# First quartet routed and sent in round 3 of attention, and GpSimd keeping at most two scattered transfers under way

## The chip, the cores and the metric

The kernel runs on one core of one Trainium2 chip. The metric is the device time of that core in microseconds, the median of several runs.

## The reference

16 sequences of 128 tokens with 128 features go through one layer of cross-attention and one layer of mixture of experts. Cut to what matters:

```python
x = x + xattn(layernorm(x), ctx, ctx, mask, Wq, Wk, Wv, Wo)   # 16 heads of 8, a softmax over 128 keys
x = x + moe(layernorm(x), wg, w1, w3, w2)                     # 8 experts, hidden size 256

# moe:
probs = softmax(x @ wg.T)
topk_w, topk_idx = top_k(probs, 2)
topk_w = topk_w / sum(topk_w)
y_e = (silu(x @ w1[e].T) * (x @ w3[e].T)) @ w2[e].T
out = sum over the two chosen experts of topk_w * y_e
```

## The kernel before, in words

**Attention.** The 16 sequences are four quartets of four. A loop over `u` from 0 to 4 runs the rounds. Round `u` starts quartet `u` (projections of queries and keys, first scores, whose row maxima VectorE takes from PSUM, L1356) and finishes quartet `u-1` (second scores with the maximum folded in, L649 and L652, exponentials on ScalarE, L905, product with the values, L627, and the projection out). Counted from 0, round 3 (`u == 3`, `u + 1 == NQ`) is the last that starts a quartet, and the last round is `u == 4`. A round has 20 ticks, `tick = 4*b + g`, with `b` from 0 to 4 and `g` from 0 to 3. Each engine's instructions are written out by hand in order of ticks, and engines meet through semaphores alone. The maxima of round `u` are turned (`MT`), copied (`mT`, L1256) and spread by GpSimd into `m_bd` (L989), which the second scores of round `u+1` read.

**Routing.** When a quartet has left attention, VectorE takes its statistics (`second_statistics`, L1043 and L1048), GpSimd the inverse deviation (`inverse_deviation`), VectorE writes the normalised rows twice each (`normalise`, L1068), TensorE turns them (`fill(("x2T", q))`) and multiplies them with the gate (`("lg", q)`), ScalarE copies (`prepare`), and VectorE ranks the experts in three steps (`routing_step`, L1154 to L1174). TensorE counts how many earlier tokens chose the same expert (`("rk", q)`, L550 and L552), `place_rows` (L1179 to L1186) turns this into row numbers, and `weigh` into weights (with `squash` on ScalarE). GpSimd then scatters the quartet's rows, eight transfers of 128 rows of 129 words, to `xg` in DRAM (`send`, L1003). The work banks of PSUM are handed round in the order of `slot_order`, built from the list `LAST_FILLS`.

**Experts.** Quartets 0 to 2 make the first phase, with 31 tiles of 128 rows, and quartet 3 the second, with 15. SyncE clears the tails of the regions (L446), waits for `sent` and loads the tiles (L464). Per tile TensorE turns it (L692), multiplies it into the hidden layer (L705 to L708), turns the result (L718) and multiplies it down (L731, L732); VectorE sums the halves into `y_sb` (`take_rows`, L1379); GpSimd scatters it to `ys` (L1016). 15 input and 14 output buffers rotate. Quartet 3 is routed while the first tiles run: from tile 8 on GpSimd sends two transfers of it after each of four tiles. Before the last round's second scores TensorE turns the first expert weights (`("W", 0)` to `("W", 3)`) and does `("rk", 0)`.

**GpSimd's order** is: `m_bd` of the round, the inverse deviations, `m_bd` of the last round, the inverse deviation of quartet 2, then the sends of quartets 0, 1 and 2, and then the tiles.

Of the kernel before, what the change touches and what calls it, by code (L numbers as in the profile page):

```python
# [47 lines left out]
QB = 4  # L48
# [35 lines left out]
def constants():  # L84
# [29 lines left out]
    for j in range(NJ):  # L114
# [10 lines left out]
LAST_FILLS = {-1: [("W", 0), ("W", 1), ("W", 2), ("W", 3), ("rk", 0)], 0: [("W", 4), ("x2T", 1)], 1: [("W", 5)], 2: [("lg", 1)],  # L125
              3: [("W", 6)], 4: [("x2T", 2)], 5: [("W", 7)], 6: [("rk", 1), ("lg", 2)], 10: [("rk", 2)], 11: [("cn", 0)],
# [8 lines left out]
def slot_order():  # L135

    order = ["w", ("cT", 0), ("xT", 0)]
    for u in range(NQ):
        order += [("V", u)]
        if u:  # L140
            order += [("MT", u - 1)]
        order += [("st", u, k) for k in range(2 * NG)]
        if u == 0:
            order += ["wo"]
        order += [("cT", u + 1), ("xT", u + 1)] if u + 1 < NQ else [("x2T", 0), ("lg", 0)]
# [25 lines left out]
def program(nc, x, ctx_in, mask, Wq, Wk, Wv, Wo, wg, w1, w3, w2, consts, xg, ys, out):  # L171
    slot, bank_of, turn, uses = slot_order()
    with ExitStack() as stack:
# [140 lines left out]
        sent = [sem(f"sent{q}") for q in range(NQ)]  # L314
# [80 lines left out]
        def _(sp):  # L395
# [43 lines left out]
            def open_phase(f):  # L439
# [10 lines left out]
                for q in (range(3) if f == 0 else range(3, NQ)):  # L450
                    sp.wait_ge(sent[q], 16 * 2 * QB)
# [28 lines left out]
        def _(pe):  # L480
# [154 lines left out]
            for u in range(NQ + 1):  # L635
                front(u)
                for b in range(QB + 1):
                    for g in range(NG):
# [39 lines left out]
                        if (b, g) == (3, 0) and u + 1 == NQ:  # L678
                            fill(("x2T", 0))
                        if (b, g) == (3, 3) and u + 1 == NQ:  # L680
                            fill(("lg", 0))
# [90 lines left out]
        def _(act):  # L772
# [76 lines left out]
            for u in range(NQ + 1):  # L849
# [31 lines left out]
                for b in range(QB + 1 if u else 0):  # L881
                    for g in range(NG):
# [6 lines left out]
                        if u == NQ:  # L889
                            for name in last_fills(NG * b + g - 1):  # L890
                                if name[0] == "W":
                                    take_weights(name[1])
                                if name[0] == "x2T":
                                    prepare(name[1])
                            if NG * b + g in (0, 5, 10):
                                squash((NG * b + g) // 5)
                        if u == NQ - 1 and (b, g) == (3, 1):
                            prepare(0)
# [48 lines left out]
        def _(pool):  # L947
# [31 lines left out]

            mask_context(0)  # L980
# [19 lines left out]
            def send(n, k):  # L1000

                f = n // QB // 3
                pool.indirect_dma_start(xg[f], bass.IndirectOffsetOnAxis(rows_i[:, n, k:k + 1], 0), sent_rows(n // QB)[:, n % QB, k, :],  # L1003
                                        None, bounds_check=E * REGS[f] - CT - 1, oob_is_err=False).then_inc(sent[n // QB], 16)

            inverse_deviation(NQ + 2)
            for q in range(3):
                pool.wait_ge(rows_ready, q + 1)
                for m in range(2 * QB):
                    send(QB * q + m // 2, m % 2)  # L1010
# [12 lines left out]

        @block.vector
        def _(dve):
# [33 lines left out]
            def normalise_batch(n0, m, b):  # L1059
                if b == 0:  # L1060
                    dve.wait_ge(rstd_ready, m + 1)
                    if m == NQ + 3:
                        dve.wait_ge(sent[0], 16 * 2 * QB)
# [185 lines left out]
            for u in range(NQ + 1):  # L1249
# [41 lines left out]
                for b in range(QB + 1):  # L1291
                    for g in range(NG):
                        if u < NQ:

                            n0, m = (QB * (u + 1), u + 1) if u + 1 < NQ else (0, NQ)
                            if (b, g) == (1, 0):
                                if u + 1 < NQ:
                                    dve.wait_ge(in_x[u + 1], 16)
                                else:
                                    dve.wait_ge(x2_done, QB)  # L1300
                            if b == 1:
                                row_statistics(n0, g)
                            if (b, g) == ((2, 0) if u + 1 < NQ else (1, 3)):
                                mean_variance(m)
                            if b == 2 and g in (1, 2) and u + 1 < NQ:
                                masks(u + 1, g - 1)
                            if b == (3 if u + 1 < NQ else 2):
                                normalise_batch(n0, m, g)
                            if u + 1 == NQ and (b, g) == (3, 0):
                                second_statistics(1)  # L1310
                            if u + 1 == NQ and b == 4:
                                if g < 3:
                                    routing_step(0, g)
                                else:
                                    normalise(QB, NQ + 1)
# [7 lines left out]
                        if u == NQ:  # L1323
# [5 lines left out]
                            if tick == 0:  # L1329
                                place_rows(0)  # L1330
                                second_statistics(2)
                            if tick == 1:
                                weigh(0)
                            if tick == 2:
                                normalise(2 * QB, NQ + 2)
                            if tick in (3, 4):
                                routing_step(1, tick - 3)
                            if tick == 5:
                                routing_step(1, 2)
                            if tick == 7:  # L1340
                                place_rows(1)
                                weigh(1)
                            if tick in (8, 9):
                                routing_step(2, tick - 8)
                            if tick == 10:
                                routing_step(2, 2)
                            if tick == 11:
                                place_rows(2)
                            if tick in (12, 13, 14):
                                table(0, tick - 12)  # L1350
                            if tick == 15:
# [91 lines left out]
```

## Time and profile before

| | |
|---|---|
| median of 3 runs | 327.69 us (327.08 to 329.23) |
| time of the profiled execution | 327.09 us |
| its span, first to last instruction | 325.3 us |
| mean granted TensorE clock | 0.871 |
| round 3 of attention (`u == 3`), its ticks | 112.6 to 142.3 us of the span |
| last round (`u == 4`) with its front | 142.3 to 202.5 us |
| expert tiles | 205.3 to 315.8 us |
| gather and output | 316 to 325.3 us |

The profiled execution took 1.8 us more than its span and 0.6 us less than the median. Times inside the kernel are counted from the start of the span. The chain of waits follows the work that ended last back to the start; what it calls another core or an unknown queue is time for which it found no releaser, and on one core there is no other core.

### The profile page before, as it was taken

What the parts mean: (1) busy time and instruction counts of PE and PEld (TensorE: products, weight loads), DVE (VectorE), ACT (ScalarE), POOL (GpSimd) and SP (SyncE); (2) the same over time, 40 slices, a digit from 0 to 9 for tenths busy, and PEclk for the clock granted to TensorE, in tenths of its full rate; (3) what the DMA queues carried; (4) which work ended last, traced back from release to release, by engine and by line L of the source; (5) the groups of instructions that cost most, each with busy time, mean ns of one, the idle gap of its engine ahead of it and who ended that gap; (6) DMA issues with size and microseconds to landing.
All of it is one profiled execution on the core that took longest, in us unless ns stands there. A gap on an engine that the chain in (4) does not pass through costs nothing.

```text
span 325.3 us, 5807 instructions
## 1 busy us (share of the span) xinstructions
PE 233.3 (72%) x1591; PEld 180.4 (55%) x1591; DVE 219.9 (68%) x642; ACT 141.8 (44%) x318; POOL 114.3 (35%) x125
## 2 busy tenths in 40 slices
PE   0946788889898988747564818679674698899820
PEld 0733565667566656546342606658563697789710
DVE  5597965887598758857734424387862586688983
ACT  6792256546655664206321406335220354455400
POOL 5201250125011502033737360035277264555540
PEclk9986599999999999957977566799985699999975
DMA  6995504450443044510301154102113134428006
GB/s 177 256 260 105 123 2 87 83 115 11 90 91 81 2 97 99 134 61 2 82 24 53 34 111 97 27 8 61 50 51 70 33 82 94 106 51 217 26 11 194
DMA packets 43886, 27.31 MB, mean 84 GB/s; under 512 B 5030, under 2 KB 41397, under 8 KB 43856
## 3 DMA queue, kind: packets, MB, share of 16 engines
q1 hardware_dynamic: 40208, 20.95, 28.2%
q0 software_dynamic: 2816, 5.27, 5.4%
q10 hardware_dynamic: 832, 0.72, 0.8%
q8 instruction: 14, 0.23, 0.3%
q14 instruction: 16, 0.13, 0.1%
HBM read 13.27 MB, written 7.37 MB: 63 GB/s over the span
## 4 chain that ended last, share of the span: by engine, by line
PE 41%; DVE 20%; issue 9%; another core or an unknown queue 8%; SPq 7%; DMA 7%; ACT 5%; POOL 2%; POOLq 0%; DVEq 0%; ACTq 0%
PE bank L493 6%; SPq L421 6%; PE bank L499 4%; DVE m_neg L1356 4%; DMA bd<-st 3%; PE bank L649 3%; PE bank L731 3%; PE bank L652 2%; PE bank L666 2%; PE bank L732 2%; PE bank L705 2%; PE bank L718 2%; PE bank L627 2%; PE bank L708 2%
## 5 line engine op out<-in xcount | busy, mean ns | idle before, releaser
L1016 POOL DMA_INDIRECT ys<-big x46 | 45.3, 986 | 41.5 <-DVE big L1379 22.6
L1356 DVE TENSOR_REDUCE m_neg<-bank 128x4 f32<-128x512 f32 x64 | 43.4, 685 | 18.1 <-PE bank L666 17.8
L905 ACT ACTIVATE big<-bank 128x512 f32<-128x512 f32 x64 | 37.5, 597 | 25.6 <-PE bank L652 24.0
L774 ACT ACTIVATE st<-bank 128x128 fp32r<-128x128 f32 (+1 forms) x92 | 26.3, 329 | 35.0 <-PE bank L718 12.9
L731 PE MATMUL bank<-bd,st 128*128 x92 | 28.1, 327 | 10.5 <-DVE big L1379 10.1
L649 PE MATMUL bank<-m_bd,ones_b 128*128 128x512 f32 x64 | 31.7, 496 | 3.7 <-ACT big L905 1.9
L666 PE MATMUL bank<-bd,st 128*128 128x512 f32 x64 | 29.1, 477 | 7.2 <-DMA bd<-st 5.8
L968 POOL TENSOR_SCALAR ve<-mv 128x4 f32<-128x4 f32 x8 | 1.8, 228 | 87.0 <-DVE mv L1048 87.0
L1398 DVE TENSOR_TENSOR big<-big,bank 128x256 f32<-128x256 f32 x46 | 19.3, 419 | 16.2 <-ACT big L937 13.6
L1283 DVE SCALAR_TENSOR_TENSOR st<-st_hi,cst,bank 128x512 fp32r<-128x512 f32 x32 | 23.3, 747 | 8.8 <-ACT st_hi L774 4.3
L937 ACT ACTIVATE big<-bank 128x256 f32<-128x256 f32 x46 | 17.7, 385 | 25.9 <-PE bank L708 13.1
L1003 POOL DMA_INDIRECT xg<-rows,rows_i x24 | 23.7, 986 | 12.2 <-issue 6.6
L705 PE MATMUL bank<-bd,st 128*128 x46 | 23.5, 510 | 6.0 <-DVE st L1367 2.9
L652 PE MATMUL bank<-bd,st 128*128 128x512 f32 x64 | 27.0, 423 | 0.0
L989 POOL TENSOR_TENSOR m_bd<-mT,cst 128x512 fp32r<-128x512 f32 x16 | 17.2, 1106 | 26.6 <-DVE mT L1256 26.6
L731 PEld LDWEIGHTS bank<-bd,st 128*128 128x128 f32 x92 | 18.2, 198 | 14.1 <-issue 12.4
L732 PE MATMUL bank<-bd,st 128*128 x92 | 24.9, 291 | 0.0
L1379 DVE TENSOR_REDUCE big<-bank 128x128 f32<-128x256 f32 x46 | 19.3, 419 | 5.8 <-remote 3.5
L1372 DVE TENSOR_TENSOR st<-bank,st 128x256 fp32r<-128x256 f32 x46 | 19.4, 422 | 4.7 <-issue 2.1
L666 PEld LDWEIGHTS bank<-bd,st 128*128 128x128 f32 x64 | 13.5, 215 | 13.2 <-issue 8.2
L774 ACT ACTIVATE onT<-bank 128x128 f32<-128x128 f32 x16 | 4.4, 276 | 37.3 <-PE bank L519 21.8
L706 PE MATMUL bank<-bd,st 128*128 x46 | 19.1, 415 | 0.0
(172 smaller groups left out, 566.4 us busy)
## 6 DMA issues: line engine op xcount, KB each, us to landing
bd<-st SPq DMA_DIRECT2D x128, 64.0 KB, 2.1
big<-xg SPq DMA_DIRECT2D x46, 64.5 KB
raw<-ys SPq DMA_DIRECT2D x8, 256.0 KB, 3.2
xg<-in_patterns SPq DMA_DIRECT2D x18, 64.5 KB
x_all<-in_x SPq DMA_DIRECT2D x4, 256.0 KB, 4.3
rows<-in_mask_BxS_if POOLq DMA_DIRECT2D x4, 256.0 KB, 5.0
ctx_all<-in_L_ffn_w SPq DMA_DIRECT2D x1, 1024.0 KB, 5.9
out<-ctx_all SPq DMA_DIRECT2D x4, 256.0 KB, 3.8
```

The lines of the kernel that those rows point to most:

```text
L649: nc.tensor.matmul(s2[k % 2][:, :], ones_b[:, b, :], m_bd[:, NJ * g:NJ * (g + 1), :].rearrange("p h q -> p (h q)"), start=True, stop=False)
L652: nc.tensor.matmul(s2[k % 2][:, :], st[:, (u - 1) % 2, 1, g, b * S:(b + 1) * S], bd_slot(0, n)[:, g, :, :].rearrange("p j q -> p (j q)"), ...
L666: nc.tensor.matmul(s1[k % s1_ring(u)][:, :], st[:, u % 2, 0, g, (b - 1) * S:b * S], bd_slot(1, n)[:, g, :, :].rearrange("p j q -> p (j q)" ...
L705: nc.tensor.matmul(both, t_lo[n % 2], first_high[:, :, bass.ds(col[n], I)], start=True, stop=False)
L731: nc.tensor.matmul(o, g_hi[n % GR][:, c * P:(c + 1) * P], w, start=(c == 0), stop=False)
L732: last = nc.tensor.matmul(o, g_lo[n % GR][:, c * P:(c + 1) * P], w, start=False, stop=(c == 1))
L774: return nc.scalar.activation(o, i, ACT.Copy)
L905: nc.scalar.activation(prob[n % 2][:, NJ * g:NJ * (g + 1), :].rearrange("p h q -> p (h q)"), s2[k % 2][:, :], ACT.Exp, scale=SCALE).then_i ...
L1003: pool.indirect_dma_start(xg[f], bass.IndirectOffsetOnAxis(rows_i[:, n, k:k + 1], 0), sent_rows(n // QB)[:, n % QB, k, :], None, bounds_ch ...
L1016: pool.indirect_dma_start(ys[f], bass.IndirectOffsetOnAxis(xt[n % XR][:, D:RW].bitcast(I32), 0), y_sb[n % YR], None, bounds_check=2 * CAPS ...
L1283: nc.vector.scalar_tensor_tensor(st[:, u % 2, is_k, g, :], st_hi[:, n % SH, :].bitcast(F32), cst[:, (C_CK if is_k else C_CQ):(C_CK if is_k ...
L1356: nc.vector.tensor_reduce(m_neg[:, H * (b - 1) + NJ * g:H * (b - 1) + NJ * (g + 1)], s1[k % s1_ring(u)][:, :].rearrange("p (j q) -> p j q" ...
```

## The change

Quartet 0's statistics move to tick 19 of round `u == 2`. Its normalisation, gate, three routing steps, count, rows and weights move to ticks 0 to 14 of round `u == 3`, and its eight transfers are issued by GpSimd there, ahead of `m_bd` of the last round. Quartet 1 comes a few ticks earlier: it is normalised at ticks 11 and 12 of `u == 3` and starts its ranking at tick 19. Quartet 2 gets its rows at tick 10 of the last round and not at tick 11. GpSimd gets waits: transfer `n` of a quartet waits until transfer `n-2` has landed, each scatter of a tile waits until that of two tiles before has landed, and quartet 3 is sent with one transfer after each of eight tiles.

```diff
-LAST_FILLS = {-1: [("W", 0), ("W", 1), ("W", 2), ("W", 3), ("rk", 0)], 0: [("W", 4), ("x2T", 1)], 1: [("W", 5)], 2: [("lg", 1)],
-              3: [("W", 6)], 4: [("x2T", 2)], 5: [("W", 7)], 6: [("rk", 1), ("lg", 2)], 10: [("rk", 2)], 11: [("cn", 0)],
+EARLY_FILLS = {4: [("x2T", 0)], 7: [("lg", 0)], 12: [("rk", 0)], 14: [("x2T", 1)], 17: [("lg", 1)]}
+LAST_FILLS = {-1: [("W", 0), ("W", 1), ("W", 2), ("W", 3)], 0: [("W", 4)], 1: [("W", 5)], 3: [("W", 6)], 4: [("rk", 1), ("x2T", 2)],
+              5: [("W", 7)], 6: [("lg", 2)], 9: [("rk", 2)], 10: [("cn", 0)],
...
-                for q in (range(3) if f == 0 else range(3, NQ)):
-                    sp.wait_ge(sent[q], 16 * 2 * QB)
+                    for k in range(2):
+                        sp.wait_ge(sent[q][k], 16 * QB)
...
+            def send(n, k):
+                f = n // QB // 3
+                if n % QB:
+                    pool.wait_ge(sent[n // QB][k], 16 * (n % QB))
+                pool.indirect_dma_start(xg[f], ...).then_inc(sent[n // QB][k], 16)
+            def send_quartet(q):
+                pool.wait_ge(rows_ready, q + 1)
+                for m in range(2 * QB):
+                    send(QB * q + m // 2, m % 2)
...
                 if u + 1 == NQ:
                     inverse_deviation(NQ)
                     inverse_deviation(NQ + 1)
+                    send_quartet(0)
             inverse_deviation(NQ + 2)
-            for q in range(3):
...
+            send_quartet(1)
+            send_quartet(2)
             inverse_deviation(NQ + 3)
             for n in range(NT):
...
+                if n >= 2:
+                    pool.wait_ge(ysb_out[(n - 2) % YR], 16 * ((n - 2) // YR + 1))
                 pool.indirect_dma_start(ys[f], ...).then_inc(ysb_out[n % YR], 16)
...
-                if 8 <= n < 8 + QB:
-                    for k in range(2):
-                        send(QB * (NQ - 1) + n - 8, k)
+                if 8 <= n < 8 + 2 * QB:
+                    send(QB * (NQ - 1) + (n - 8) // 2, n % 2)
...
+                            if u + 2 == NQ and (b, g) == (4, 3):
+                                second_statistics(0)
+                            if u + 1 == NQ:
+                                tick = NG * b + g
+                                if b == 0:
+                                    normalise_batch(0, NQ, g)
+                                if tick == 5:
+                                    second_statistics(1)
+                                if tick in (8, 9, 10):
+                                    routing_step(0, tick - 8)
+                                if tick in (11, 12):
+                                    for k in (0, 1):
+                                        normalise_batch(QB, NQ + 1, 2 * (tick - 11) + k)
+                                if tick == 13:
+                                    place_rows(0)
+                                if tick == 14:
+                                    weigh(0)
+                                if tick == 19:
+                                    routing_step(1, 0)
...
                             if tick == 0:
-                                place_rows(0)
                                 second_statistics(2)
-                            if tick == 1:
-                                weigh(0)
-                            if tick == 2:
+                            if tick in (1, 2):
+                                routing_step(1, tick)
+                            if tick == 3:
                                 normalise(2 * QB, NQ + 2)
-                            if tick in (3, 4):
-                                routing_step(1, tick - 3)
                             if tick == 5:
-                                routing_step(1, 2)
-                            if tick == 7:
                                 place_rows(1)
                                 weigh(1)
```

## Rows read from the trace of the kernel before

**Rows 1.** The page, busy time by engine and the chain's shares.

```profile
PE 233.3 (72%) x1591; PEld 180.4 (55%) x1591; DVE 219.9 (68%) x642; ACT 141.8 (44%) x318; POOL 114.3 (35%) x125
...
PE 41%; DVE 20%; issue 9%; another core or an unknown queue 8%; SPq 7%; DMA 7%; ACT 5%; POOL 2%; POOLq 0%; DVEq 0%; ACTq 0%
```

**Rows 2.** The chain in order of time: start, length, what.

```profile
162.19 3.04 another core or an unknown queue
...
172.22 7.61 another core or an unknown queue
...
186.15 9.01 another core or an unknown queue
...
242.89 3.46 another core or an unknown queue
...
249.26 4.26 another core or an unknown queue
```

**Rows 3.** Timeline of the last round: start, length, engine, line, idle before.

```profile
153.32 1.12 POOL L1003 DMA_INDIRECT xg<-rows,rows_i  x1 [0.19 <-issue]
...
162.49 0.97 POOL L1003 DMA_INDIRECT xg<-rows,rows_i  x1 [0.31 <-issue]
...
173.41 0.33 PE L519 MATMUL bank<-cst,on 128*128 128x128 f32 x1
...
177.34 0.97 POOL L1003 DMA_INDIRECT xg<-rows,rows_i  x1 [0.30 <-issue]
...
179.84 0.28 ACT L774 ACTIVATE onT<-bank 128x128 f32<-128x128 f32 x1 [7.05 <-remote]
```

**Rows 4.** Stretches of the last round: PE, PEld, DVE, ACT, POOL busy, clock, DMA.

```profile
161.60:165.30 3.70, 1.42 (x6) 0.78 (x5) 0.15 (x1) 0.64 (x3) 1.56 (x2) 1.00 0.12 39
165.30:173.50 8.20, 6.75 (x51) 4.87 (x50) 4.99 (x18) 3.08 (x6) 4.01 (x4) 0.58 0.08 26
```

**Rows 5.** DMA engines' busy tenths, 173 to 181 us in 40 slices.

```profile
DMA  1001700000800000450000090000072000000000
```

**Rows 6.** The chain, last scatter to its landing.

```profile
313.74 2.09 DMA ys<-big
```

**Rows 7.** Stretches of round u == 3, columns as in Rows 4.

```profile
112.60:117.30 4.70, 3.84 (x15) 2.18 (x14) 2.27 (x4) 3.87 (x7) 0.00 (x0) 1.00 0.35 72
117.30:132.40 15.10, 13.87 (x151) 10.10 (x150) 12.37 (x38) 8.20 (x17) 2.53 (x4) 1.00 0.48 97
132.40:142.30 9.90, 3.49 (x45) 2.28 (x44) 9.18 (x33) 0.61 (x3) 0.00 (x0) 0.82 0.51 141
```

**Rows 8.** Timeline, VectorE's steps of statistics, ranking and placing.

```profile
133.30 0.43 DVE L1158 TENSOR_TENSOR cT<-cT,cst 128x256 f32<-128x256 f32 x1
...
149.47 0.19 DVE L1179 TENSOR_TENSOR place<-bank,cst 128x32 f32<-128x32 f32 x1 [0.32 <-PE bank L552]
...
150.21 0.17 DVE L1186 CAST rows_i<-m_hl 128x8 int32<-128x8 f32 x1
...
150.41 0.87 DVE L1043 BATCH_NORM_STATS2 stats<-x_all 128x6 f32<-128x128 f32 x4
```

**Rows 9.** Timeline, GpSimd's spreading of the maxima ahead of the last round.

```profile
143.21 4.03 POOL L989 TENSOR_TENSOR m_bd<-mT,cst 128x512 fp32r<-128x512 f32 x4 [13.04 <-DVE mT L1256]
```

**Rows 10.** The chain at the start of the last round.

```profile
148.60 0.41 PE bank L550 x2
149.01 0.42 PE bank L552 x2
```

**Rows 11.** DMA issues, the load of w2 beside round u == 3.

```profile
ctx_all<-in_L_ffn_w SPq DMA_DIRECT2D x1, 1024.0 KB, 5.9
```

**Rows 12.** L1379 alone by stretch: length, busy (count of tiles), clock, DMA.

```profile
216.00:236.00 20.00, 3.34 (x8) 0.96 0.18 49
236.00:255.50 19.50, 1.68 (x4) 0.68 0.22 53
...
262.00:305.00 43.00, 10.46 (x25) 1.00 0.42 103
```

More of the change, by code:

```diff
@@ L144, in slot_order @@
             order += ["wo"]
-        order += [("cT", u + 1), ("xT", u + 1)] if u + 1 < NQ else [("x2T", 0), ("lg", 0)]
+        order += [("cT", u + 1), ("xT", u + 1)] if u + 1 < NQ else [name for tick in EARLY_FILLS for name in EARLY_FILLS[tick]]
     order += [("MT", NQ - 1)]
@@ L313, in program @@
         rows_ready, wgt_ready = sem("rows_ready"), sem("wgt_ready")
-        sent = [sem(f"sent{q}") for q in range(NQ)]
+        sent = [[sem(f"sent{q}_{k}") for k in range(2)] for q in range(NQ)]
         tab_ready = sem("tab_ready")
@@ L677, in _ @@
                             transpose_tokens(u + 1)
[L678 to L681, printed above, removed]
+                        if u + 1 == NQ:
+                            for name in EARLY_FILLS.get(NG * b + g, []):
+                                fill(name)
                         if u == NQ:
@@ L894, in _ @@
                                     prepare(name[1])
[L895 to L898, printed above, removed]
+                            if NG * b + g in (3, 10):
+                                squash(1 if b == 0 else 2)
+                        if u == NQ - 1:
+                            if (b, g) in ((1, 1), (3, 3)):
+                                prepare(b // 2)
+                            if (b, g) == (3, 0):
+                                squash(0)
                         if b < QB:
@@ L1062, in normalise_batch @@
                     if m == NQ + 3:
-                        dve.wait_ge(sent[0], 16 * 2 * QB)
+                        dve.wait_ge(sent[0][0], 16 * QB)
+                        dve.wait_ge(sent[0][1], 16 * QB)
                     if m >= NQ:
@@ L1293, in _ @@
                         if u < NQ:
-                            n0, m = (QB * (u + 1), u + 1) if u + 1 < NQ else (0, NQ)
-                            if (b, g) == (1, 0):
-                                if u + 1 < NQ:
+                            n0, m = QB * (u + 1), u + 1
+                            if u + 1 < NQ:
+                                if (b, g) == (1, 0):
                                     dve.wait_ge(in_x[u + 1], 16)
-                                else:
-                                    dve.wait_ge(x2_done, QB)
@@ L1301, in _ @@
[L1301 to L1315, printed above, removed]
+                                if b == 1:
+                                    row_statistics(n0, g)
+                                if (b, g) == (2, 0):
+                                    mean_variance(m)
+                                if b == 2 and g in (1, 2):
+                                    masks(u + 1, g - 1)
@@ new lines, in _ @@
+                                if b == 3:
+                                    normalise_batch(n0, m, g)
+                            if u + 2 == NQ and (b, g) == (4, 3):
+                                second_statistics(0)
+                            if u + 1 == NQ:
+                                tick = NG * b + g
[14 more added lines that the diff above has]
+                                    routing_step(1, 0)
@@ L1329, in _ @@
                             if tick == 0:
-                                place_rows(0)
                                 second_statistics(2)
-                            if tick == 1:
-                                weigh(0)
-                            if tick == 2:
+                            if tick in (1, 2):
+                                routing_step(1, tick)
+                            if tick == 3:
                                 normalise(2 * QB, NQ + 2)
-                            if tick in (3, 4):
-                                routing_step(1, tick - 3)
                             if tick == 5:
-                                routing_step(1, 2)
-                            if tick == 7:
                                 place_rows(1)
                                 weigh(1)
-                            if tick in (8, 9):
-                                routing_step(2, tick - 8)
+                            if tick in (7, 8, 9):
+                                routing_step(2, tick - 7)
                             if tick == 10:
-                                routing_step(2, 2)
-                            if tick == 11:
                                 place_rows(2)
-                            if tick in (12, 13, 14):
-                                table(0, tick - 12)
-                            if tick == 15:
+                            if tick in (11, 12, 13):
+                                table(0, tick - 11)
+                            if tick == 14:
                                 weigh(2)
```

9 lines of the change are left out of this document (2 added, 7 removed).

## Prediction

> **What bounds the kernel now.** I read the page first. TensorE is busy 72% of the span and leads the chain with 41%, VectorE has 20%, GpSimd only 2% [rows 1]. So nothing is saturated, and GpSimd's transfers look free. The odd share is 8% "another core or an unknown queue", on a kernel of one core. The chain in order of time says where it lies: five pieces, three in the last round and two in the expert phase, 3.04 + 7.61 + 9.01 + 3.46 + 4.26 = 27.4 us [rows 2]. I then laid the timeline of the last round beside them. GpSimd issues eight transfers back to back from 153.32 to 162.49, (162.49 - 153.32) / 7 = 1.31 us apart. The second burst's last goes out at 177.34. TensorE's L519 starts at 173.41 and takes 0.33, yet ScalarE, which waits for nothing else, copies its result at 179.84, 6.1 us late [rows 3]. A third burst goes the same way, with the wait from 186.15 to 195.2 [rows 2]. Each long wait begins 4 to 9 us into a burst and ends 1 to 2 us after the last scatter's own instruction; none lies where the scatters have gaps. I call this the stall: something TensorE has done, or should do, isn't seen while GpSimd scatters without a pause. Why, the trace doesn't show. Behind a stall the clock is at half: granted share 0.58 over 165.3 to 173.5, after 3.7 us in which TensorE was busy 1.4 [rows 4].
>
> **Part by part**, against the profiled execution's own 327.09 us.
>
> *Statistics of quartet 0 in round 2's tick 19.* Four instructions, 0.87 us, and their gathering, 0.38 by the same view of another quartet: +1.2 us [rows 8]. They stand ahead of that round's last maximum, where VectorE has no pause, so I count them whole. In round 3 they are saved from the sum below.
>
> *Round 3.* VectorE is busy 2.27 of 4.70 us, then 12.37 of 15.10, then 9.18 of 9.90 [rows 7]. The last stretch, ticks 16 to 19, is its ranking and the second normalisation, with TensorE busy a third of it. The ranking moves to ticks 8 to 10 and the normalising of quartet 0 into ticks 0 to 3, where 2.4 us were idle. VectorE's work over the 29.7 us is 23.8; it loses 1.25 (statistics) and gains placing, 149.47 to 150.38 = 0.9, weighing, three instructions of that kind, 0.6, and the first ranking step, two of 0.43 and a small one, 1.1 [rows 8]. That makes 25.2. With some 2 us of idle time left, where 5.9 was, the maxima are ready at 112.6 + 25.2 + 2 = 139.8, or 2.5 us sooner; bounds 0 and -4. Together with the 1.2 above: -1.3.
>
> *Quartet 0's burst in round 3.* Rows are placed at tick 13, about 131 us, so eight transfers run to 142 and land by 144. By the pattern a stall begins 4 to 7 us in and ends near 144. The maxima, due at 141.0, then come at about 144.5, against 142.3 before. So the burst costs +3.5 here; bounds 0 (everything TensorE owes was seen before) and +8.5 (the longest such wait, nearly [rows 2]). GpSimd's `m_bd` of the last round is queued behind the burst. Its four instructions began at 143.21, took 4.03, and the first scores needing them came right after `rk` 0, at 149.4 [rows 9, 10]. So five microseconds of delay are covered by the turning of the weights; a start at 145 costs nothing, one at 149 would cost 3.
>
> *The wait for the transfer before last.* A scatter lands 2.09 us after its issue [rows 6], and two intervals are 2.6. The DMA strip shows separate pulses with idle slices between them: each transfer's packets are over before the next one's start [rows 5]. So the limit of two is kept already, and I price the waits at nothing, with bounds of 0 and +3 us for a round in which landing is late. Late it may be in round 3: the 1 MB load of w2 is issued at 134.7 and takes 5.9 us [rows 11]. The waiting instruction has `m_bd` behind it, which has the cover just named. The Trainium skill, "DMA: Bandwidth & Descriptors", section "Queues, rings and completion order", says that a completion increment lands only after every earlier write of that DMA engine, whatever its queue. By it a scatter issued beside the w2 load would land up to 5.9 us late rather than 2.1, and one wait would last 3.3 us; that uses up the upper bound just given and stays under the cover. No row of before shows a scatter beside that load.
>
> *Start of the last round.* `rk` 0 goes from between the weights and the first scores: 0.41 + 0.42 = 0.8 us of the chain [rows 10]: -0.8. In ticks 0 to 4 VectorE loses placing, weighing and the first ranking step, 0.9 + 0.6 + 1.1 = 2.6, of a stretch that it mostly bounds: -2.0, bounds 0 and -2.6.
>
> *The first stall of the last round* goes with its burst: -3.7, and of the 8.2 us at 0.58 of the clock behind it, with TensorE busy 6.75, about a third of the busy time: -2.0 [rows 4]. Bounds for both -2 and -7, since quartet 1's burst now starts two ticks earlier.
>
> *The second and third bursts* stay back to back: 0.
>
> *Quartet 3 in the expert phase.* Before it tiles take 20.0 / 8 = 2.5 us, during it 19.5 / 4 = 4.9, later 43 / 25 = 1.7 [rows 12]. So it costs 19.5 - 4 x 2.5 = 9.5 us. With one transfer per tile GpSimd needs 2 x 1.31 = 2.6 us for each of eight tiles, nearly as long as a tile takes, and still scatters without a pause. But a stall starves it: no tile, no scatter, and its queue is empty after one or two pieces, where before up to two sends and a tile stood ready each time. I take half: -4.5, bounds 0 and -9.5. The rings of 14 and 15 buffers cover GpSimd's lag of 8 x (2.6 - 2.0) = 5 us. The wait on the tile scatter before last is met, since two tiles take 3.4 us and landing 2.1.
>
> **Sum.** -1.3 + 3.5 - 0.8 - 2.0 - 3.7 - 2.0 - 4.5 = -10.8, so 316.3; with the 0.6 us by which the median lies above the profiled execution, 316.9. I say 317.
>
> **Rivals.**
> 1. *The stalls vanish* because no third transfer is ever under way. For it: all five lie in unbroken bursts, and the longest, 9.01, lies where SyncE clears the regions, whose copies may make landings late [rows 2]. Against it: by rows 5 and 6 there is no third transfer to hold back in the second burst, which stalls as long. It would give the sum without the +3.5, and the second and third stall, 7.61 + 9.01 less some 1.3 us of ordinary work in each = 14, with 5 more in the expert phase and 4 of clock: 316.9 - 3.5 - 14 - 5 - 4 = 290, and up to 303 where other waits take half of that over. Taken at 295.
> 2. *It moves, nothing more.* The stall of burst one costs in round 3 what it cost in the last round, the clock's dip goes with it, and quartet 3's sends stall for as long as before. The sum is then -1.3 + 5.7 - 0.8 - 2.0 - 5.7 - 0 = -4.1 with the parts as taken, and 0 at their weak ends: 323 to 331, taken at 326.
> 3. *Slower: GpSimd's queue in round 3.* The burst with its waits runs beside the block-diagonal copies and w2. If landing takes the 5.9 us of the load for two of the eight and 3.4 for others, the burst ends near 149 rather than 142, `m_bd` starts 6 us late and the first scores come some 4 us late, with a stall of 8.5 in front of the maxima. Then -1.3 + 8.5 + 4 - 0.8 - 2.0 - 3.7, with no gain at quartet 3 and none of clock, is +4.7: 332. It decides once the last transfer ends later than about 147 us of the span.
>
> **Chances.** Forecast 0.54 (309 to 323), stalls vanish 0.16, moves only 0.17, slower 0.13. A difference of 1%, 3.3 us, is about what a measurement of this kernel can tell from none. Faster by over 1% (under 324.4): 0.54 + 0.16 + 0.04 = 0.74; within 1%: 0.13; slower by over 1% (over 331.0): 0.13. The range 297 to 328 leaves out the slow case and the lower part of the first rival, 0.13 + 0.06. It is wide because the stall's cause isn't known.
>
> **What would show it.** In the changed profile: eight scatters of quartet 0 between about 131 and 143 us, still 1.3 us apart, and a long unexplained wait that ends within 2 us of the last one; no wait on `m_bd`; the last round's first scores at 148 to 150 us; two and not three long waits behind it; the first expert tile near 197 and not 205 us; eight tiles of quartet 3's sending at 3 us each. The prediction is wrong if unbroken bursts run without a stall, if the waits stretch the bursts well over 1.4 us a transfer, or if the stall blocks round 3's maxima for its whole length.

## The result, and the profile after

The changed kernel took 318.63 us (median of 4 runs, 317.59 to 321.41), the kernel before beside it 328.46 us (4 runs, 327.08 to 329.5). The ratio is 0.9727, 95% interval 0.9689 to 0.9765: faster by 2.7%. (A ratio can differ by some tenths of a per cent from the quotient of the two medians.) Forecast were 317.0 us, 297 to 328. The number is right, but in part by luck: it stands on two errors that cancel, and in another set of runs the same two kernels came out the other way (told under the experiments).

The page after, busy time and the chain's shares, answers to [rows 1]:

```profile
PE 233.2 (74%) x1591; PEld 179.9 (57%) x1591; DVE 220.1 (70%) x642; ACT 141.8 (45%) x318; POOL 114.0 (36%) x125
...
PE 38%; DVE 20%; DMA 13%; issue 12%; SPq 8%; POOL 5%; ACT 2%; another core or an unknown queue 2%; POOLq 0%; DVEq 0%; ACTq 0%
```

No engine works less. What changed is the chain: unknown time falls from 8% to 2%, DMA rises from 7% to 13% and GpSimd from 2% to 5%. The chain in order of time has these unknown pieces left, where [rows 2] had 27.4 us in five:

```profile
230.83 2.02 another core or an unknown queue
...
241.05 1.74 another core or an unknown queue
...
250.25 1.01 another core or an unknown queue
```

All three lie in the expert phase; none is left in attention. What stands there instead is GpSimd's throttled queue. The chain from round 3's end to the first expert tile, start, length, what:

```profile
139.05 5.41 DMA xg<-rows,rows_i
...
149.31 1.07 POOL m_bd L1006
150.52 0.77 PE bank L651
...
164.84 0.73 issue
165.57 0.57 POOL xg L989
...
177.41 2.97 DMA xg<-raw,rows_i
...
181.16 3.81 DMA xg<-raw,rows_i
...
187.03 2.29 DMA xg<-raw,rows_i
189.67 1.80 DMA big<-xg
...
192.84 0.46 PE bank L693
```

Read it from the bottom up: the first expert tile (L693, 192.84) needs its gather, the gather needs the last transfer of quartet 2 (187.03), and that one waited for the transfer before last, and so on. Quartet 0's burst in GpSimd's timeline shows where the wait bites; the bracket is the idle time before the instruction:

```profile
135.94 1.00 POOL L989 DMA_INDIRECT xg<-rows,rows_i  x1 [0.30 <-issue]
137.75 0.97 POOL L989 DMA_INDIRECT xg<-rows,rows_i  x1 [0.80 <-issue]
139.05 0.97 POOL L989 DMA_INDIRECT xg<-rows,rows_i  x1 [0.34 <-issue]
...
145.25 0.97 POOL L989 DMA_INDIRECT xg<-rows,rows_i  x1 [3.23 <-DMA xg<-rows,rows_i]
...
148.33 0.97 POOL L989 DMA_INDIRECT xg<-rows,rows_i  x1 [0.81 <-DMA xg<-rows,rows_i]
149.31 4.03 POOL L1006 TENSOR_TENSOR m_bd<-mT,cst 128x512 fp32r<-128x512 f32 x4
```

Idle times of 0.30 and 0.80 take turns, so a pair of transfers takes 3.1 us and not 2.56. The transfer of 139.05, issued while w2 was loading, landed 5.41 us on and held the next but one for 3.23. `m_bd` (L1006) started at 149.31, not 143.21 [rows 9], and TensorE's first scores had to wait for it:

```profile
150.52 0.77 PE L651 MATMUL bank<-m_bd,ones_b 128*128 128x512 f32 x1 [1.13 <-POOL m_bd L1006]
```

The first expert tile comes at 192.84 where it came at 205.26: -12.4 us. The last scatter of a tile starts at 304.16 against 313.74 [rows 6]: -9.6. So attention won more than the kernel did, and the expert phase lost 2.8. The windows, for the reduction that each tile does once (L1394, [rows 12]'s L1379), show length, busy time with the count of tiles, clock, DMA:

```profile
205.00:224.00 19.00, 2.93 (x7) 0.94 0.19 51
224.00:252.00 28.00, 3.80 (x9) 0.85 0.24 61
252.00:295.00 43.00, 9.61 (x23) 0.96 0.37 96
```

While quartet 3 is sent, a tile takes 28.0 / 9 = 3.1 us; afterwards 43 / 23 = 1.87, against 1.72 in [rows 12].

### The profile page after: what moved, and what is told of

The parts are those of the page before. It is cut to its first block, busy times and chain, and to the rows that moved or that the text cites. A ratio compares the mean times of both kernels' runs of the same rounds, so it can differ in the third digit from the quotient of the medians.

```text
span 315.8 us, 5812 instructions
## 1 busy us (share of the span) xinstructions
PE 233.2 (74%) x1591; PEld 179.9 (57%) x1591; DVE 220.1 (70%) x642; ACT 141.8 (45%) x318; POOL 114.0 (36%) x125
## 3 DMA queue, kind: packets, MB, share of 16 engines
q1 hardware_dynamic: 40208, 20.95, 28.2%
## 4 chain that ended last, share of the span: by engine, by line
PE 38%; DVE 20%; DMA 13%; issue 12%; SPq 8%; POOL 5%; ACT 2%; another core or an unknown queue 2%; POOLq 0%; DVEq 0%; ACTq 0%
SPq L422 7%; PE bank L495 6%; POOL xg L989 5%; DMA bd<-st 4%; PE bank L732 4%; DVE m_neg L1371 4%; PE bank L733 4%; PE bank L706 3%; PE bank L709 3%; DMA xg<-raw,rows_i 3%; PE bank L707 3%; PE bank L719 2%; PE bank L501 2%; PE bank L668 2%; DMA w_nat<-in_L_xattn_Wv 2%
## 5 line engine op out<-in xcount | busy, mean ns | idle before, releaser
L909 ACT ACTIVATE big<-bank 128x512 f32<-128x512 f32 x64 | 37.6, 597 | 21.1 <-PE bank L654 20.9
L732 PE MATMUL bank<-bd,st 128*128 x92 | 27.8, 322 | 13.1 <-DVE big L1394 12.0
L651 PE MATMUL bank<-m_bd,ones_b 128*128 128x512 f32 x64 | 30.5, 476 | 4.3 <-ACT big L909 1.9
L706 PE MATMUL bank<-bd,st 128*128 x46 | 24.1, 523 | 5.0 <-DVE st L1382 3.1
L733 PE MATMUL bank<-bd,st 128*128 x92 | 25.4, 296 | 0.0
L1394 DVE TENSOR_REDUCE big<-bank 128x128 f32<-128x256 f32 x46 | 19.3, 421 | 6.4 <-remote 4.1
L1006 POOL TENSOR_TENSOR m_bd<-mT,cst 128x512 fp32r<-128x512 f32 x16 | 17.3, 1109 | 14.7 <-DVE mT L1268 14.7
L668 PEld LDWEIGHTS bank<-bd,st 128*128 128x128 f32 x64 | 13.8, 220 | 14.1 <-issue 9.2
L707 PE MATMUL bank<-bd,st 128*128 x46 | 19.4, 422 | 0.0
L651 PEld LDWEIGHTS bank<-m_bd,ones_b 128*128 128x128 f32 x64 | 12.9, 202 | 11.3 <-issue 6.5
```

Of the source, the lines that this page charges most:

```text
L651: nc.tensor.matmul(s2[k % 2][:, :], ones_b[:, b, :], m_bd[:, NJ * g:NJ * (g + 1), :].rearrange("p h q -> p (h q)"), start=True, stop=False)
L668: nc.tensor.matmul(s1[k % s1_ring(u)][:, :], st[:, u % 2, 0, g, (b - 1) * S:b * S], bd_slot(1, n)[:, g, :, :].rearrange("p j q -> p (j q)" ...
L706: nc.tensor.matmul(both, t_lo[n % 2], first_high[:, :, bass.ds(col[n], I)], start=True, stop=False)
L707: nc.tensor.matmul(both, t_hi[n % 2], first_high[:, :, bass.ds(col[n], I)], start=False, stop=False)
L732: nc.tensor.matmul(o, g_hi[n % GR][:, c * P:(c + 1) * P], w, start=(c == 0), stop=False)
L733: last = nc.tensor.matmul(o, g_lo[n % GR][:, c * P:(c + 1) * P], w, start=False, stop=(c == 1))
```

## Experiments

Two theories at first. *The limit*: keeping a third scattered transfer from being under way removes the stalls, and the new order adds little. *The order*: less work beside the bursts removes them, and the waits are free, as the prediction had it. The first eight kernels ran in two sets, beside the kernel before at 327.66 us (13 runs) and 329.45 us (13 runs).

**The limit taken away, the order kept.** All waits between transfers go:

```diff
-                if n % QB:
-                    pool.wait_ge(sent[n // QB][k], 16 * (n % QB))
...
-                if n >= 2:
-                    pool.wait_ge(ysb_out[(n - 2) % YR], 16 * ((n - 2) // YR + 1))
```

> The new order of routing and sending, with both new waits of GpSimd left out. Theory A (the limit inserts a pause of some 0.5 us after every second transfer, and the long unexplained waits end in it): the long waits of 4 to 9 us come back with every burst of eight, and the time is 323 to 330 us. Theory B (the prediction's: the limit is never reached and the order makes the gain): 316 to 320 us, bursts 1.3 us apart, long waits as in the changed kernel.

Measured: 325.82 us (10 runs), ratio 0.9924 [0.9885, 0.9963]. Its chain has the long pieces again, two of the longest:

```profile
139.19 7.18 another core or an unknown queue
...
187.22 7.90 another core or an unknown queue
```

The transfers run 1.28 us apart; quartet 0's go out from 134.59 to 143.71, and the maxima of round 3 wait until 146.4, 2.7 us after the last of them. So the order alone moves the first stall into round 3 and leaves a long one in the third burst (the second has 1.45 and 1.36); it is worth 0.8%.

**The limit alone, on the kernel before.** Only the wait between a quartet's sends is added there:

```diff
+                if n % QB:
+                    pool.wait_ge(sent[n // QB][k], 16 * (n % QB))
```

> The kernel before with its old order, and only the wait for the transfer before last in each send of a quartet. Theory A: the three long waits of the last round shrink to 1 to 3 us each, 314 to 320 us. Theory B: nothing to see, 326 to 330 us with the same three waits.

Measured: 320.99 us (4 runs), 0.9756 [0.9699, 0.9812]. One unknown piece is left, 1.95 us at 237.28. The wait that the prediction priced at nothing makes by itself a gain that can't be told from the whole one (the intervals overlap). What the order adds to it is seen in the waits (engine, line, for whom: us in total, times, longest) and in the chain of this kernel:

```profile
PEld bank L693 <- DMA big<-xg: 13.1, 2, 12.7
```

```profile
193.61 2.29 DMA xg<-raw,rows_i
...
196.25 1.86 DMA big<-xg
```

The three bursts run from 154.24 to 193.61, the last transfer is issued at 193.61, and TensorE stands idle for it. In the changed kernel it is issued at 187.03 and TensorE's idle time before the first tile is 2.8; the tile comes at 192.84 and not 198.16. The new order starts the longer queue earlier; that is its use. Of these 5.3 us the last scatter of a tile keeps 3.4 (304.16 against 307.53); the limit alone has no wait between the tiles' scatters.

**The tile's wait taken away**, the sends' kept:

```diff
-                if n >= 2:
-                    pool.wait_ge(ysb_out[(n - 2) % YR], 16 * ((n - 2) // YR + 1))
```

> The changed kernel without the wait of a tile's scatter for that of two tiles before; the sends keep theirs. If the wait is met anyway, as predicted: within 1% of the changed kernel, 317 to 320 us. If it holds up the expert phase: 2 to 4 us less. If it gives pauses that end long waits there too: 2 to 5 us more, with longer waits between tiles 8 and 16.

Measured: 317.78 us (4 runs), 0.9679 [0.9613, 0.9744]. Its unknown pieces are 2.74, 1.71 and 1.00, as in the changed kernel. So the wait between tiles' scatters removes no stall. The changed kernel's 0.9727 lies inside this interval, so a gain from leaving the wait out isn't shown in the time. In the profile the stretch behind quartet 3's sends is shorter, 52.1 us against 55.0 (taken up below under Quartet 3).

**w2 loaded behind the block-diagonal copies:**

```diff
                     if not k and u >= 1:
                         block_diagonal(0, QB * (u - 1) + b)
+                if u == NQ:
+                    sp.wait_ge(work_full, slot["cT", NQ - 1] + 1)
+                    sp.dma_start(raw[2].rearrange("p (e i) -> p e i", e=E), w2.rearrange("e h i -> h e i")).then_inc(in_w2, 16)
```

(and its two lines go from ahead of them.)

> The changed kernel with the 1 MB load of w2 issued behind the last block-diagonal copies of the last round instead of ahead of that round. Theory C (in round 3 the load makes two scatters land late, GpSimd waits for them, and m_bd behind them is on the path): the eight transfers of quartet 0 end some 4 us earlier, m_bd starts near 145, 314 to 317 us. Theory D (something else is late next, or the load now hits quartet 1's transfers): 317 to 321 us.

Measured: 320.08 us (4 runs), 0.9711 [0.9642, 0.9781]; profiled 321.07. The late landing is gone, the burst's last transfer comes at 146.03 and not 148.33, and `m_bd` starts at 147.02. In its place the chain has an unknown 3.32 us at 139.49, beside quartet 0's burst, and four pieces of 8.3 us together in the expert phase (4.8 in the changed kernel). So that the load makes a landing late is confirmed, and that it costs the kernel anything is not. The 3.32 also show that two under way don't rule a stall out.

**What in the wait does it?** The landing, so that no third transfer is under way, or the gap of 0.80 us that the wait leaves? Four kernels replace the wait between sends; the tiles' wait stays.

*A short pause, no wait*: a memset on GpSimd before every second transfer.

```diff
-                if n % QB:
-                    pool.wait_ge(sent[n // QB][k], 16 * (n % QB))
+                if n % QB and k == 0:
...
+                    nc.gpsimd.memset(spare[:, 170 * (slot_n % 6):170 * (slot_n % 6 + 1)], 0.0)
```

> The changed kernel with the sends' waits replaced by a short memset of GpSimd on spare columns ahead of every second transfer (about 0.2 us plus its issue), so that nothing waits for a landing. Theory P (any pause of GpSimd between two transfers lets TensorE's work be seen): 316 to 321 us, no long wait over 4 us. Theory Q (a transfer must have landed and nothing may be in flight behind it): as without the limit, 323 to 327 us, with waits of 7 to 9 us.

Measured: 332.67 us (4 runs), 1.0112 [1.0048, 1.0175]. GpSimd's timeline in its third burst, and the chain's longest piece:

```profile
183.11 0.97 POOL L991 DMA_INDIRECT xg<-raw,rows_i  x1 [0.30 <-issue]
184.07 0.26 POOL L990 MEMSET ws_lo<- 128x170 f32 x1
184.50 0.97 POOL L991 DMA_INDIRECT xg<-raw,rows_i  x1 [0.16 <-issue]
```

```profile
184.44 9.97 another core or an unknown queue
```

The memset fills time that was idle anyway; a pair takes 2.66 us and not 3.1. So it was too short to test what a longer pause does. It shows that another instruction between the transfers doesn't remove the stalls.

*A wait that is already met*:

```diff
-                    pool.wait_ge(sent[n // QB][k], 16 * (n % QB))
+                    pool.wait_ge(rows_ready, n // QB + 1)
```

> The changed kernel with the sends' waits put on a semaphore that has long been reached (the quartet's rows). Theory P: transfers stay 1.28 us apart with no pause, and the long waits are back, 323 to 327 us. If a wait instruction alone breaks the issue: 317 to 320 us.

Measured: 332.08 us (10 runs), 1.0094 [1.0059, 1.013]; unknown pieces of 7.28 and 8.28 us in attention. A wait instruction that finds its semaphore met doesn't remove them either.

*One transfer under way*:

```diff
-                if n % QB:
-                    pool.wait_ge(sent[n // QB][k], 16 * (n % QB))
+                if k:
+                    pool.wait_ge(sent[n // QB][0], 16 * (n % QB + 1))
+                elif n % QB:
+                    pool.wait_ge(sent[n // QB][1], 16 * (n % QB))
```

> The changed kernel with at most one scattered send under way (each waits for the one before). Theories P and Q: no unexplained wait above 1.5 us, but 2.3 to 2.6 us per transfer, so a burst of eight takes 18 to 20 us; m_bd starts near 153 and the first expert tile waits for the last send: 320 to 328 us.

Measured: 351.28 us (4 runs), 1.0691 [1.0606, 1.0776]. The chain has no unknown piece at all, and GpSimd takes 3.1 us for each transfer:

```profile
155.66 0.97 POOL L991 DMA_INDIRECT xg<-rows,rows_i  x1 [2.11 <-DMA xg<-rows,rows_i]
158.77 0.97 POOL L991 DMA_INDIRECT xg<-rows,rows_i  x1 [2.14 <-DMA xg<-rows,rows_i]
```

The last send goes out at 223.84, and the first tile comes at 228.3. Here the limit's price is seen without any stall against it.

*Three under way*, with three semaphores per quartet:

```diff
-                if n % QB:
-                    pool.wait_ge(sent[n // QB][k], 16 * (n % QB))
+                m = 2 * (n % QB) + k
+                if m >= 3:
+                    pool.wait_ge(sent[n // QB][m % 3], 16 * (m // 3))
```

> The changed kernel with at most three sends under way. Two intervals of 1.28 plus one more are 3.8 us and a landing takes 2.1, so no wait holds except beside the w2 load. Theory P: as without the limit, 322 to 327 us, waits of 7 to 9 us back in the last round. If the count in flight matters by itself: between the changed kernel and that, 318 to 322 us.

Measured: 333.09 us (5 runs), 1.0123 [1.0062, 1.0184]. The five fall into two groups, 326.25 and 330.47, and three of 333.09 to 333.92, so whether it is slower than the kernel before (329.45) stays unclear; a gain like that of the limit of two isn't there. The wait holds a transfer up in two places, beside the w2 load and for two transfers of the third burst:

```profile
147.44 0.97 POOL L990 DMA_INDIRECT xg<-rows,rows_i  x1 [3.84 <-DMA xg<-rows,rows_i]
...
191.40 0.97 POOL L990 DMA_INDIRECT xg<-raw,rows_i  x1 [1.79 <-DMA xg<-raw,rows_i]
```

Elsewhere the transfers are 1.28 us apart. Attention has unknown pieces of 5.87 us in the first burst and 1.50 and 1.34 in the second, and none in the third, where the order alone had 7.90. By its profile (326.25 us, the quickest of its runs) it is no better than the order alone (324.83). So of the three limits only two gains anything. One costs too much, and three seldom holds anything back.

The short pause, the met wait and three under way lie about 1% above the kernel before, the order alone 0.8% below it. They ran in another set, and they keep the tiles' wait, which the order alone leaves out: from tile 16's scatter to tile 45's they take 58.1, 54.7 and 55.3 us, the order alone 50.4.

**The set that came out otherwise.** Four more kernels were meant to settle whether the landing or the length of the pause counts, and to find a better version. In this set the kernel before took 304.17 us (11 runs, 301.26 to 308.98), some 24 us less than in the sets until then. The set holds the changed kernel itself:

> The changed kernel itself, on the same chip as the other three, as their measure: 317 to 320 us.

Measured: 314.5 us (6 runs), 1.0362 [1.0286, 1.0437]: the changed kernel is 3.6% *slower* than the one before. Its profile has no unknown piece, though seventeen scatters of quartet 3 and the tiles run without a break, from 226.82 to 247.23 with 1.28 us between them:

```profile
226.82 0.96 POOL L989 DMA_INDIRECT xg<-rows,rows_i  x1 [0.81 <-DVE rows_i L1198]
228.09 0.97 POOL L1028 DMA_INDIRECT ys<-big  x1 [0.30 <-issue]
229.36 0.97 POOL L989 DMA_INDIRECT xg<-rows,rows_i  x1 [0.30 <-issue]
...
247.23 0.97 POOL L1028 DMA_INDIRECT ys<-big  x1 [0.30 <-issue]
```

In the first profile of this kernel the same stretch has unknown pieces at 230.83 and 241.05, and scatters 3.3 and 3.5 us apart behind them; from tile 8's scatter to tile 45's it took 304.16 - 223.89 = 80.3 us there and 298.64 - 225.05 = 73.6 here. So unbroken scattering doesn't always bring the stall. Where it stays away, only the price of the two waits is left. The sends':

```profile
PEld bank L693 <- DMA big<-xg: 15.0, 3, 11.9
```

TensorE waits 11.9 us for the last sends. The tiles': the last sum of a tile ends at 292.50, and its scatter, held by those before it, starts 6.1 us later.

```profile
292.08 0.42 DVE L1394 TENSOR_REDUCE big<-bank 128x128 f32<-128x256 f32 x1 [1.01 <-PE bank L733]
...
298.64 0.97 POOL L1028 DMA_INDIRECT ys<-big  x1 [0.31 <-issue]
```

In every kernel without this wait at the end the same distance is 0.8 us. The 24 us by which the kernel before is quicker are close to the 27.4 us of its five unknown pieces [rows 2], and 304 is close to the upper end of the 290 to 303 that the first rival gave for vanished stalls. The kernel before wasn't profiled in this set, so that its stalls were absent is inferred from its time and from these four profiles, none of which has an unknown piece.

**A longer pause, no wait for landing:**

```diff
-                if n % QB:
-                    pool.wait_ge(sent[n // QB][k], 16 * (n % QB))
+                if n % QB and k == 0:
+                    own(nc.gpsimd.memset(ve[:, :], 0.0))
```

> The changed kernel with the sends' waits replaced by a tiny memset of GpSimd ahead of every second transfer, for whose end GpSimd waits before it issues on. No landing is waited for, but the pause between transfers is at least as long as with the limit (0.8 us or more where it was 0.3). Theory P (a pause of that length is what lets TensorE's work be seen): 316 to 321 us and no unexplained wait over 4 us. Theory Q (only a wait for a landing helps): 323 to 333 us, waits of 7 to 9 us as with the shorter pause.

Measured: 311.43 us (4 runs), 1.0268 [1.0194, 1.0342]; a pair takes 3.17 us, no unknown piece.

```profile
165.46 0.12 POOL L988 MEMSET ve<- 128x4 f32 x1
166.37 0.97 POOL L989 DMA_INDIRECT xg<-rows,rows_i  x1 [0.80 <-POOL ve L988]
```

It was meant to tell a pause from a landing. In a set without stalls it can't, and that stays open. It is 3.1 us under the changed kernel, with intervals that overlap. What it does show: 0.80 us pass between the end of the memset and the next transfer, the same 0.80 as behind a landing in the changed kernel.

**Two under way over both kinds**, while quartet 3 is sent:

```diff
+                if n // QB == NQ - 1:
+                    if k:
+                        pool.wait_ge(sent[n // QB][0], 16 * (n % QB + 1))
+                    elif n % QB:
+                        pool.wait_ge(sent[n // QB][1], 16 * (n % QB))
+                elif n % QB:
                     pool.wait_ge(sent[n // QB][k], 16 * (n % QB))
...
-                if n >= 2:
-                    pool.wait_ge(ysb_out[(n - 2) % YR], 16 * ((n - 2) // YR + 1))
+                if 9 <= n <= 8 + 2 * QB:
+                    pool.wait_ge(ysb_out[(n - 1) % YR], 16 * ((n - 1) // YR + 1))
```

> The changed kernel with the limit of two kept over both kinds of transfer while quartet 3 is sent: each of its sends waits for the send before, each tile's scatter in that stretch for the tile before, and no other tile waits. Theory: the unexplained waits of 1 to 2 us between tiles 8 and 16 go, with the clock's dips behind them, and that stretch falls from 28 to some 24 us: 313 to 316 us. Rival: GpSimd now needs 3 us and more for each of eight tiles, and the stretch stays as long: 317 to 320 us.

Measured: 316.14 us (6 runs), 1.0397 [1.0322, 1.0471], not told from the changed kernel's 314.5. About stalls it says nothing, as there was none to remove. Its profile shows the rival of the expectation: from tile 8's scatter to tile 16's it takes 27.4 us against 20.9. Without the wait behind that stretch GpSimd catches up, and its last scatter starts 0.8 us behind the sum and not 6.1; so the loss and the gain about cancel.

**Quartet 0 routed early, but sent behind `m_bd` of the last round:**

```diff
                 if u + 1 == NQ:
...
-                    send_quartet(0)
+            send_quartet(0)
             inverse_deviation(NQ + 2)
```

> The changed kernel with quartet 0 routed as early, but sent behind m_bd of the last round. Theory C (m_bd behind the burst costs some 1 to 3 us, and the burst slows round 3): m_bd starts near 145 and the last round 2 to 4 us sooner. Theory E (GpSimd's 24 transfers in a row set the end of the last round, since the first tile waits for the last one): the first expert tile comes 6 to 10 us later, 324 to 328 us. E is the likelier.

Measured: 320.55 us (4 runs), 1.0527 [1.0441, 1.0614]. The first tile comes at 201.8 and not 194.2, 7.6 us later, with 12.0 us of waiting for the last sends. So sending in round 3 is worth 320.55 - 314.5 = 6.05 us in this set. What routing there is worth without it wasn't tested.

With stalls, the four kernels that keep sends at two under way lie from 0.968 to 0.976, with intervals that overlap; without them, the kernel before leads all that ran. The new order without either wait didn't run in the last set, so whether it would lead there is open.

## Why the prediction was right, point by point

**The stall.** What the prediction called the stall is real and was rightly tied to unbroken scattering, in the sets that had it. In attention the longest piece is 5.87 to 9.97 us in all five kernels whose sends run mostly unbroken (the one before, the order alone, the short pause, the met wait, three under way); with two or one under way the longest there is 3.32. In the expert phase sends and tiles' scatters run 1.28 us apart in the changed kernel too, and with two of either kind allowed pieces of up to 4.22 us remain. (One reading of the prediction was off: the third long wait begins not 4 but 186.15 - 183.41 = 2.7 us into its burst.)

**The step that failed: the waits of two, priced at nothing.** "Two intervals are 2.6" and "a scatter lands 2.09 us after its issue", "so the limit of two is kept already". Both numbers nearly held (2.56 and 2.29 here); the conclusion left out what passes between the landing and the next start. The chain shows it as 0.73 us of issue behind every second transfer. So the wait costs (3.1 - 2.56) / 2 = 0.27 us a transfer, about 6.5 over 24 of them. Late landings come on top: between the first and last start of the two runs of sends lie 13.8 + 24.6 = 38.4 us, where 22 intervals of 1.28 make 28.2, some 10 us less. In return the wait removes the long stalls. The first rival's argument against itself was the same step. With the stalls present its mechanism, not the forecast's, is what happened; its time of 290 to 303 didn't come: the throttled sends, which now end last before the first tile, took part of the gain back. Limit alone 0.9756, order alone 0.9924, both 0.9727.

**Second and third bursts, priced at 0.** From the first scores to the first tile, before took 205.26 - 149.4 = 55.9 us, after 192.84 - 150.52 = 42.3: -13.6, where the steps for that stretch gave -2.0 - 3.7 - 2.0 = -7.7. The missing 5.9 us fit the pieces of 7.61 and 9.01 [rows 2], which are gone, less what the throttled queue took back; how the rest divides no run shows.

**Round 3, -2.5.** VectorE's work came out as foretold, 25.23 us where the sum had 25.2, over a stretch of 30.4 us (113.8 to 144.2). But it was idle for 5.2 us of that and not for 2. So the gain at the maxima didn't come: the last was taken by 143.48, against 141.67 before, with no long stall ahead of it, where the sum without a stall had it 1.3 us sooner. The 2 us of idle time left were an estimate; no row gave them.

**Quartet 0's burst, +3.5.** It was expected as a stall ahead of the maxima and as nothing at `m_bd`. It came the other way: no stall, but `m_bd` at 149.31, the end of the cover at "149 would cost 3", past the 147 from which the third rival decides. It cost less than that rival said, as the scores waited 1.13 us only: they need the first of `m_bd`'s four instructions (1.07 us), not all 4.03. First scores at 150.52 against 149.4 before, +1.1; the steps up to there gave -1.3 + 3.5 - 0.8 = +1.4. The burst began at 134.5 and not 131, since the rows were placed at 133.4.

**The w2 load.** This is as the prediction's bound had it: the transfer beside it landed 5.41 us on, and one wait lasted 3.23. The Trainium skill, "DMA: Bandwidth & Descriptors", section "Queues, rings and completion order", has the rule from which the prediction worked out a landing up to 5.9 us late and a wait of 3.3, and the trace agrees: 5.41 and 3.23. With the load moved away the long landing was gone.

**Quartet 3, -4.5.** By the scatters of tiles 8 to 16 the stretch took 249.12 - 223.89 = 25.2 us, at 3.15 each as foretold, against 263.30 - 235.95 = 27.4 before: -2.1. The rest went the other way: tiles 16 to 45 took 304.16 - 249.12 = 55.0 against 313.74 - 263.30 = 50.4, +4.6. Without the tiles' wait they took 303.02 - 250.97 = 52.1. The kernels with the new order bear it out, all but one: with the tiles' wait this stretch takes 55.0 (w2 later), 54.7, 55.3 and 58.1 us, without it 52.1 and 50.4; with one send under way, though, it takes 50.6 in spite of the wait. So the wait, priced as met, is not always met. Two tiles take 3.4 us, and landing (2.1) with the start behind it (0.80) takes 2.9, which leaves little to spare; in the set without stalls the scatters end 6.1 us behind. Here it looks to cost some 3 us, 55.0 - 52.1, but in the time of the kernel (0.9679 against 0.9727) it can't be told.

**Sum.** Attention -12.4 for -6.3, experts +2.8 for -4.5: -9.6 for -10.8. The two misses are 6.1 one way and 7.3 the other, and that they nearly cancel is luck.

**What stays open.** What TensorE's results are held by. Whether the landing or the longer gap frees them: the changed kernel's three unknown pieces end at 232.85, 242.79 and 251.26, which is 2.09, 2.26 and 2.14 us after the start of the last scatter ahead of their end, about its time to landing [rows 6]; that speaks for the landing, but no run parts the two. And what differs between the sets with stalls and the one without. The second set and this one ran on the same chip, so the chip alone doesn't decide. The verdict of 2.7% holds where the stalls are.

## What to carry to other kernels

A wait that by durations is already met can still cost if it sits between back-to-back instructions: add the time from the semaphore to the next start before pricing it at nothing, here 0.80 us. When a chain has unexplained pieces that lie inside one queue's unbroken bursts, test the throttle by itself, in both directions (none, one, two, three under way), and count how much later the queue ends and who waits for its end. And take the kernel before again in each set: here its time moved by 24 us, and with it the sign of the change.

## What the chip did that was not expected

- Between a landing (or any work waited for) and the next scatter on GpSimd lie 0.73 to 0.80 us, against 0.30 between unwaited ones. One scatter under way takes 3.1 us each, two 1.55, unlimited 1.28.
- TensorE's finished results stayed unseen for up to 9.97 us while scatters were issued 1.28 to 1.39 us apart; with pairs of sends 3.1 us apart for 4.98 at most (changed kernel, up to 182.64), and with one under way no such wait is left. In the expert phase, where both kinds of scatter run 1.28 us apart, it was up to 5.4 even with the limit (ScalarE at L938, limit alone). A met wait and a memset between them didn't help.
- The same kernel took 329.45 us in one set and 304.17 in another on the same chip, and scatters 1.28 us apart held nothing up in the second.
- The mean granted clock of the profiled executions doesn't simply follow the stalls. It is 0.871 before and 0.889 after, and 0.891 for the changed kernel in the set without them. But it is 0.869 with the limit alone and 0.862 with one under way, which have hardly any unknown piece, and 0.879 with the short pause, which has the longest.
